# Moving two small statistics operations from VectorE to GpSimd in a graph network kernel

## The chip, the cores and the metric

The kernel runs on one core of one Trainium2 chip. The core has TensorE (matmuls), VectorE and ScalarE (elementwise work, reductions and activations), GpSimd (elementwise work as well, without access to the matmuls' accumulators) and SyncE, which starts the transfers here. Each engine has its own queue of instructions and works through it in order; the engines wait for one another through semaphores. The metric is the time of one execution on the device, in microseconds (us).

## What is computed

128 graphs of 128 nodes with 256 features each go through a first normalisation and three layers of attention over the neighbours, each followed by a feed-forward block; the input is added at the end. Cut to what matters:

```python
def layernorm(x, gamma, beta):
    mu = jnp.mean(x, axis=-1, keepdims=True)
    var = jnp.var(x, axis=-1, keepdims=True)
    return (x - mu) * jax.lax.rsqrt(var + EPS) * gamma + beta
mask = adjacency_matrix.astype(jnp.float32) + jnp.eye(n, dtype=jnp.float32) > 0
x = node_features                      # relu of a plain layernorm of the input
for l in range(attn_w.shape[0]):       # 3 layers
    si = x @ attn_w[l, :d]
    sj = x @ attn_w[l, d:]
    scores = si[:, :, None] + sj[:, None, :] + attn_b[l]
    scores = jnp.where(scores >= 0, scores, 0.2 * scores)
    scores = jnp.where(mask, scores, -jnp.inf)
    attn = jax.nn.softmax(scores, axis=-1)
    agg = jnp.einsum('bij,bjd->bid', attn, x)
    h = layernorm(x + agg, g1[l], beta1[l])
    ff = jax.nn.gelu(h @ W1[l] + b1[l], approximate=False) @ W2[l] + b2[l]
    x = layernorm(h + ff, g2[l], beta2[l])
return x                               # the kernel adds the input to it
```

There are three normalisations: of the input (number 0 in the code), after the attention (1) and after the feed-forward block (2). Each needs, per node, a mean and a variance, then (variance + epsilon) to the power -1/2 and minus the mean times that.

## The kernel before, in words

Four graphs form a group (T = 4), so that a tile is 128 nodes by 4 graphs by 256 features. An item is one group in one layer: 32 groups by 3 layers make 96 items, ordered so that four groups go through the three layers together (12 items to a round of the loop). The program is a software pipeline of slots. In slot s, TensorE runs the feed-forward block of item s in eight pieces (c = 0 to 7), and in between the other stages of its neighbours: the aggregation of item s+1, the transposes of its normalised rows (L435), the attention scores and the transposes of the probabilities of item s+2 (L413). The other engines have a list for each slot, written out by hand in the functions `slot`, with the same eight pieces; nothing reorders it. In four slots out of twelve a new group comes in as item s+4 and its statistics and its mask are made there too.

What the change touches is the way from rows to a normalised tile. VectorE makes statistics of each row (`statistics`, L580, `bn_stats`), and a piece later `aggregates` (L582): four `bn_aggr` (one per graph, L585) that leave mean and variance in `mv`, then one operation that adds epsilon to the variances (`var_eps`, L587) and one that negates the means (`minus_mean`, L588). Both read and write 128x4 numbers in SBUF. Then GpSimd's `inverse_deviation` (L786) raises to the power -1/2 (L789, `rstd`) and multiplies (L791, `shift`). ScalarE (numbers 0 and 1, L491) or GpSimd itself (number 2, `norm_feed`, L815) applies `rstd` and `shift` to the rows.

VectorE calls `aggregates` in three places of a slot: for the attention's norm of item s+1 at c == 0, ahead of the `g_lo` of piece 1 (L573) and the dot products of item s+2 (`dot_products`, L614 and L617); for the feed-forward norm of item s-1 at c == 4, behind the scores (L632), the row maxima (L638) and `minus_max` (L642) of item s+2; and, where a group comes in, for the input's norm at c == 6, ahead of the mask (L601, L604). `feed_residual` at c == 2 makes `res2` (L681).

GpSimd's list in a slot is `inverse_deviation` 1, `h_residual` (L801, L803: two operations on 128x1024 that wait for `norm1`, the dot products and `res2`), `low_X` (L807, `X_lo`), `inverse_deviation` 2, `norm_feed` (four of L815), in some slots the addition of the input to a finished result (`skip_connection`, L836), `inverse_deviation` 0 where a group comes in, and `layer_output` (L827 and L829, two of each).

ScalarE's list has GELU (L481) and the half-precision copy `g_hi` (L486) of each piece, `norm1` (L491) behind piece 2, the copy `X_hi` behind piece 3, the copy of the transposed rows behind piece 4, and behind piece 5 `leaky` (L509) and the exponentials (L514), which wait for `minus_max`.

Of the kernel before, what the change touches and what calls it, by code (L numbers as in the profile page):

```python
# [27 lines left out]
ALU = mybir.AluOpType  # L28
# [101 lines left out]
def gnn_kernel(nc, x, adj, attn_w, attn_b, W1, b1, W2, b2, g1, beta1, g2, beta2, out):  # L130
    with ExitStack() as ctx:
# [335 lines left out]
        def _(act):  # L467
# [26 lines left out]
            def norm_input(r, s):  # L494
                act.wait_ge(rstd_ready[0], group_total(r, s, 2, 2))


                norm_apply(s, 0, x_in[s % 2], X[s % RING], ACT.Relu, x0_ready)

            def norm_attention(r, s):  # L500
                act.wait_ge(rstd_ready[1], total(r, s, 2, 2))
                if later(r, s):
                    act.wait_ge(nT_psum, total(r, s - 1, 1, 1))
                    act.wait_ge(h_res_steps, total(r, s - 1, 2, 2))
                norm_apply(s, 1, res1, norm1, ACT.Identity, norm1_ready)
# [55 lines left out]
        def _(dve):  # L561
# [19 lines left out]

            def aggregates(n, after_8):  # L582

                for t in range(T):
                    dve.bn_aggr(mv[n][:, t, :], bn[n][:, t, :]).then_inc(stat_steps[n], 1)  # L585
                dve.wait_ge(stat_steps[n], after_8)
                dve.tensor_scalar(var_eps[n][:], mv[n][:, :, 1], EPS, None, ALU.add).then_inc(stat_steps[n], 1)  # L587
                dve.tensor_scalar(minus_mean[n][:], mv[n][:, :, 0], -1.0, None, ALU.mult).then_inc(stat_steps[n], 1)  # L588

            def input_statistics(r, s):  # L590
                dve.wait_ge(x_loaded[s % 2], lane_total(r, s))
                if later(r, s):
                    dve.wait_ge(rstd_ready[0], group_total(r, s, 2, 0))
                statistics(0, x_in[s % 2])
# [111 lines left out]
            def slot(r, s):  # L706
# [7 lines left out]
                for c in range(C):  # L714

                    if c == 0 and is_item(r, s + 1):
                        dve.wait_ge(stat_steps[1], total(r, s + 1, 10, 4))
                    if c == 4 and is_item(r, s - 1):
                        dve.wait_ge(stat_steps[2], total(r, s - 1, 10, 4))
                    if c == 6 and starts and not late:  # L720
                        dve.wait_ge(stat_steps[0], group_total(r, s + 4, 10, 4))
                    if isinstance(r, int) and (r, s, c) == (0, -2, 3):
                        dve.wait_ge(stat_steps[0], group_total(0, 1, 10, 4))
                    if is_item(r, s):
                        hidden(r, s, c)
                    if c == 0 and is_item(r, s + 1):
                        aggregates(1, total(r, s + 1, 10, 8))
                    if c == 2 and is_item(r, s - 1):
# [8 lines left out]
                    if isinstance(r, int) and (r, s, c) == (0, -2, 3):  # L737
                        aggregates(0, group_total(0, 1, 10, 8))
                    if c == 3 and is_item(r, s - 1):
# [6 lines left out]
                    if c == 4 and is_item(r, s - 1):  # L746
                        aggregates(2, total(r, s - 1, 10, 8))
                    if c == 5 and is_item(r, s + 1):
# [5 lines left out]
                    if c == 6 and starts and not late:  # L754
                        aggregates(0, group_total(r, s + 4, 10, 8))
                    if c == 6 and is_item(r, s + 2):
# [16 lines left out]
        def _(pool):  # L773
# [12 lines left out]
            def inverse_deviation(s, n, count_stats, count_rstd):  # L786

                pool.wait_ge(stat_steps[n], count_stats)
                pool.tensor_tensor(rstd[n][s % 2][:], var_eps[n][:], minus_half[:], ALU.pow).then_inc(rstd_ready[n], 1)  # L789
                pool.wait_ge(rstd_ready[n], count_rstd)  # L790
                pool.tensor_tensor(shift[n][s % 2][:], minus_mean[n][:], rstd[n][s % 2][:], ALU.mult).then_inc(rstd_ready[n], 1)  # L791
# [17 lines left out]
            def norm_feed(r, s):  # L809

                pool.wait_ge(rstd_ready[2], total(r, s, 2, 2))
                if later(r, s):
                    pool.wait_ge(x_steps, x_total(r, s - 1, 4))
                for t in range(T):
                    pool.tensor_scalar(norm2[:, t, :], res2[:, t, :], rstd[2][s % 2][:, t:t + 1], shift[2][s % 2][:, t:t + 1],  # L815
                                       ALU.mult, ALU.add).then_inc(norm2_ready, 1)
# [21 lines left out]
            def slot(r, s):  # L838
# [3 lines left out]
                if is_item(r, s + 1):  # L842
                    inverse_deviation(s + 1, 1, total(r, s + 1, 10, 10), total(r, s + 1, 2, 1))
                    h_residual(r, s + 1)
                if is_item(r, s + 2):
                    low_X(r, s + 2)
                if is_item(r, s - 1):
                    inverse_deviation(s - 1, 2, total(r, s - 1, 10, 10), total(r, s - 1, 2, 1))
                    norm_feed(r, s - 1)
                if is_item(r, s - 2) and layer_of(s - 2) == L - 1:  # L850
                    skip_connection(r, s - 2)
                if is_item(r, s + 4) and layer_of(s + 4) == 0:
                    inverse_deviation(s + 4, 0, group_total(r, s + 4, 10, 10), group_total(r, s + 4, 2, 1))
                if is_item(r, s - 1) and not (isinstance(r, int) and PER * r + s == ITEMS):
# [24 lines left out]
```

## Time and profile before

| what | value |
|---|---|
| median of three runs | 2462.75 us (2460.89 to 2462.85) |
| the profiled execution's own time | 2464.22 us |
| its span, first to last instruction | 2462.4 us |
| mean granted clock of TensorE | 0.993 of full speed |
| TensorE busy | 2350.7 us, 95% of the span |
| VectorE busy | 2097.8 us, 85% |
| ScalarE busy | 1890.0 us, 77% |
| GpSimd busy | 1701.0 us, 69% |
| transfers, mean rate | 29 GB/s |

The profile is of one execution. Its span leaves out what lies before the first and after the last instruction, 1.8 us here. Busy time is the time in which an instruction of the engine is under way, waiting for a port included; time in which the engine waits for a semaphore is idle time. Engines are named PE (TensorE), DVE (VectorE), ACT (ScalarE), POOL (GpSimd) and SP (SyncE); L12 is line 12 of the program, and an operation is given as output<-inputs by the program's names. Times in the timelines are microseconds from the start of the span.

### The profile page before, as it was taken

To read this page: it belongs to the slowest core of one execution; us is meant where nothing else is said; L and a number is where in the kernel's file an instruction comes from. 1 tells how busy PE (TensorE), PEld (TensorE's weight loads), DVE (VectorE), ACT (ScalarE), POOL (GpSimd) and SP (SyncE) were. 2 spreads that over 40 slices of the span, in tenths; PEclk is the share of its full clock that TensorE was granted. 3 is DMA by queue.
4 is the path that set the end of the run, shared out by engine and by line. 5 is a ranking of instruction groups with operands and counts; after the bars stand their busy time and mean duration, and the time that the engine had idled before them with its cause. 6 is when DMAs were issued, how large, how long until landed. Compare 5 with 4: busy or idle time off the path is not lost.

```text
span 2462.4 us, 47718 instructions
## 1 busy us (share of the span) xinstructions
PE 2350.7 (95%) x16608; PEld 1648.4 (67%) x16608; DVE 2097.8 (85%) x6070; ACT 1890.0 (77%) x3402; POOL 1701.0 (69%) x1540
## 2 busy tenths in 40 slices
PE   3999999999999999999999999999999999999997
PEld 2766666676666666667666666666666666666765
DVE  6778998888988899888988889988898889988884
ACT  4767788877787878787787777877778777878783
POOL 3457677767776767766786667776678676777675
PEclk9999999999999999999999999999999999999998
DMA  5200012000210002100021001200012000110001
GB/s 170 73 1 1 1 44 78 1 1 1 74 48 1 1 14 61 48 1 1 14 78 31 1 1 31 73 18 2 1 44 61 18 2 1 44 52 1 1 1 52
DMA packets 77422, 70.84 MB, mean 29 GB/s; under 512 B 7040, under 2 KB 75648, under 8 KB 77184
## 3 DMA queue, kind: packets, MB, share of 16 engines
q1 hardware_dynamic: 77184, 67.79, 9.1%
q8 instruction: 134, 2.20, 0.4%
q14 instruction: 104, 0.85, 0.1%
HBM read 51.01 MB, written 16.78 MB: 28 GB/s over the span
## 4 chain that ended last, share of the span: by engine, by line
DVE 55%; PE 19%; ACT 13%; issue 10%; POOL 0%; DVEq 0%; POOLq 0%
DVE g_lo L573 11%; DVE bn L580 9%; PE p_pair L383 8%; DVE res L656 6%; DVE dots L614 6%; ACT probs L514 5%; PE p_hid L369 5%; ACT L514 5%; DVE res L681 5%; DVE scores L632 4%; DVE dots L617 4%; PE p_pair L425 3%; DVE row_top L638 3%; DVE minus_max L642 2%; PE p_att L413 2%
## 5 line engine op out<-in xcount | busy, mean ns | idle before, releaser
L383 PE MATMUL p_pair<-w_hi,g_hi 128*128 128x256 f16 x3072 | 839.1, 273 | 0.0
L383 PE MATMUL p_pair<-w_lo,g_hi 128*128 128x256 f16 x3072 | 838.8, 273 | 0.0
L383 PE MATMUL p_pair<-w_hi,g_lo 128*128 128x256 f16 x3072 | 838.8, 273 | 0.0
L481 ACT ACTIVATE p_hid<-p_hid,b_eff 128x512 f32<-128x512 f32 x768 | 504.5, 657 | 328.6 <-PE p_hid L369 327.4
L573 DVE TENSOR_TENSOR g_lo<-p_hid,g_hi 128x512 f16<-128x512 f32 x768 | 527.5, 687 | 239.4 <-ACT g_hi L486 232.9
L801 POOL TENSOR_TENSOR h_res<-norm,g_rows 128x1024 f32<-128x1024 f32 x96 | 227.7, 2372 | 395.8 <-DVE res L681 389.1
L486 ACT ACTIVATE g_hi<-p_hid 128x512 f16<-128x512 f32 x768 | 458.5, 597 | 24.3
L369 PE MATMUL p_hid<-hT_hi,w_hi 128*128 128x512 f16 x1536 | 458.7, 380 | 2.3 <-DVE g_lo L573 2.3
L369 PE MATMUL p_hid<-hT_hi,w_lo 128*128 128x512 f16 x1536 | 458.9, 380 | 0.0
L369 PE MATMUL p_hid<-hT_lo,w_hi 128*128 128x512 f16 x1536 | 458.8, 380 | 0.0
L789 POOL TENSOR_TENSOR rstd<-var_eps,minus_half 128x4 f32<-128x4 f32 x224 | 241.6, 1079 | 307.4 <-DVE minus_mean L588 302.1
L383 PEld LDWEIGHTS p_pair<-w_lo,g_hi 128*128 128x128 f16 x3072 | 301.2, 98 | 107.3 <-issue 0.8
L383 PEld LDWEIGHTS p_pair<-w_hi,g_hi 128*128 128x128 f16 x3072 | 301.2, 98 | 106.2 <-issue 1.0
L383 PEld LDWEIGHTS p_pair<-w_hi,g_lo 128*128 128x128 f16 x3072 | 301.2, 98 | 35.5
L491 ACT ACTIVATE norm<-res,shift,rstd 128x256 f32<-128x256 f32 x384 | 199.3, 589 | 102.0 <-POOL shift L791 102.0
L369 PEld LDWEIGHTS p_hid<-hT_lo,w_hi 128*128 128x128 f16 x1536 | 150.8, 98 | 182.6 <-issue 2.5
L369 PEld LDWEIGHTS p_hid<-hT_hi,w_lo 128*128 128x128 f16 x1536 | 150.7, 98 | 182.5 <-issue 2.2
L580 DVE BATCH_NORM_STATS2 bn<-res 128x6 f32<-128x256 f32 x768 | 268.9, 414 | 3.3
L803 POOL TENSOR_TENSOR h_res<-h_res,res_rows 128x1024 f32<-128x1024 f32 x96 | 226.9, 2363 | 7.5
L587 DVE TENSOR_SCALAR var_eps<-mv 128x4 f32<-128x4 f32 x224 | 213.4, 953 | 7.7
L815 POOL TENSOR_SCALAR norm<-res,rstd,shift 128x256 f32<-128x256 f32 x384 | 209.8, 561 | 10.0
L656 DVE SCALAR_TENSOR_TENSOR res<-p_pair,row_inv,X 128x256 f32<-128x256 f32 x384 | 159.0, 477 | 65.5 <-PE p_pair L425 65.5
(67 smaller groups left out, 3855.2 us busy)
## 6 DMA issues: line engine op xcount, KB each, us to landing
x_in<-in_x SPq DMA_DIRECT2D x32, 512.0 KB, 5.3
x_again<-in_x SPq DMA_DIRECT2D x32, 512.0 KB, 5.1
out<-y_out SPq DMA_DIRECT2D x32, 512.0 KB, 3.3
adj_in<-in_adj SPq DMA_DIRECT2D x32, 256.0 KB, 5.6
w_f<-in_L_gnn_W SPq DMA_DIRECT2D x6, 1024.0 KB, 5.6
attn_rows<-in_L_gnn_attn_w SPq DMA_DIRECT2D x1, 768.0 KB, 5.6
g_rows<-in_L_gnn_g SPq DMA_DIRECT2D x2, 384.0 KB, 8.3
b_rows<-in_L_gnn_b SPq DMA_DIRECT2D x1, 384.0 KB, 7.4
```

The lines of the kernel that those rows point to most:

```text
L369: mm = pe.matmul(p_hid[in_ring(s, c, PF_RING)][:], w[l][:, k, cols], h[i][:, k, :], start=(n == 0), stop=(n == 3 * KD - 1))
L383: mm = pe.matmul(ff_banks(s)[:, t, :], g[i][:, nodes], w[l][:, c, :], start=(c == 0 and t % 2 == 0 and n == 0), stop=(c == C - 1 and n == ...
L481: act.activation(p_hid[k][:], p_hid[k][:], ACT.Gelu, bias=b1_eff[:, l, c:c + 1], scale=1.0 / WSCALE).then_inc(gelu_ready, 1)
L486: act.activation(g_hi[i][:], p_hid[k][:], ACT.Copy).then_inc(g_hi_ready, 1)
L514: act.activation(probs[:, t, :], leaky[:, t, :], ACT.Exp, bias=minus_max[:, t:t + 1], accum_out=row_sum[:, t:t + 1]).then_inc(probs_ready, 1)
L573: dve.tensor_tensor(g_lo[i][:], p_hid[k][:], g_hi[i][:], ALU.subtract).then_inc(g_lo_ready, 1)
L580: dve.bn_stats(bn[n][:, t, :], src[:, t, :]).then_inc(stat_steps[n], 1)
L587: dve.tensor_scalar(var_eps[n][:], mv[n][:, :, 1], EPS, None, ALU.add).then_inc(stat_steps[n], 1)
L656: dve.scalar_tensor_tensor(out=res1[:, t, :], in0=agg_banks(s)[:, t, :], scalar=row_inv[:, t:t + 1], in1=X[s % RING][:, t, :], op0=ALU.mul ...
L789: pool.tensor_tensor(rstd[n][s % 2][:], var_eps[n][:], minus_half[:], ALU.pow).then_inc(rstd_ready[n], 1)
L801: pool.tensor_tensor(h_res[i][:], norm1[:], rows(g1_rows, l, T), ALU.mult).then_inc(h_res_steps, 1)
L803: pool.tensor_tensor(h_res[i][:], h_res[i][:], rows(res_rows, l, T), ALU.add).then_inc(h_res_steps, 1)
```

## The change

The two operations behind the aggregation move from VectorE's `aggregates` to GpSimd's `inverse_deviation`, ahead of the power. VectorE's part ends with `bn_aggr`; its semaphore `stat_steps` counts 8 steps per use instead of 10, and GpSimd's `rstd_ready` counts 4 instead of 2, since GpSimd now waits for its own two operations before it raises to the power. All other waits keep their meaning with the new counts.

```diff
@@ VectorE
-            def aggregates(n, after_8):
+            def aggregates(n):
                 for t in range(T):
                     dve.bn_aggr(mv[n][:, t, :], bn[n][:, t, :]).then_inc(stat_steps[n], 1)
-                dve.wait_ge(stat_steps[n], after_8)
-                dve.tensor_scalar(var_eps[n][:], mv[n][:, :, 1], EPS, None, ALU.add).then_inc(stat_steps[n], 1)
-                dve.tensor_scalar(minus_mean[n][:], mv[n][:, :, 0], -1.0, None, ALU.mult).then_inc(stat_steps[n], 1)
@@ GpSimd
             def inverse_deviation(s, n, count_stats, count_rstd):
                 pool.wait_ge(stat_steps[n], count_stats)
+                pool.tensor_scalar(var_eps[n][:], mv[n][:, :, 1], EPS, None, ALU.add).then_inc(rstd_ready[n], 1)
+                pool.tensor_scalar(minus_mean[n][:], mv[n][:, :, 0], -1.0, None, ALU.mult).then_inc(rstd_ready[n], 1)
+                pool.wait_ge(rstd_ready[n], count_rstd - 1)
                 pool.tensor_tensor(rstd[n][s % 2][:], var_eps[n][:], minus_half[:], ALU.pow).then_inc(rstd_ready[n], 1)
@@ counts, one of each kind
-                act.wait_ge(rstd_ready[1], total(r, s, 2, 2))
+                act.wait_ge(rstd_ready[1], total(r, s, 4, 4))
-                        dve.wait_ge(stat_steps[1], total(r, s + 1, 10, 4))
+                        dve.wait_ge(stat_steps[1], total(r, s + 1, 8, 4))
-                    inverse_deviation(s + 1, 1, total(r, s + 1, 10, 10), total(r, s + 1, 2, 1))
+                    inverse_deviation(s + 1, 1, total(r, s + 1, 8, 8), total(r, s + 1, 4, 3))
```

On VectorE, between the aggregation of the attention's norm (c == 0) and the dot products, this stood before (ISA is the instruction of a dot product and of the read of its sum):

```order
L580 BN_STATS bn<-res 128x6 x3
L573 TENSOR_TENSOR g_lo<-p_hid,g_hi 128x512 [waits g_hi_ready,stat_steps1]
L585 BN_AGGR mv<-bn 128x2 x4
L587 TENSOR_SCALAR var_eps<-mv 128x4 [waits stat_steps1]
L588 TENSOR_SCALAR minus_mean<-mv 128x4
L573 TENSOR_TENSOR g_lo<-p_hid,g_hi 128x512 [waits g_hi_ready]
L614 ISA dots,s_i<-X,attn_rows,attn_b_col 128x256 [waits x_steps]
```

and this stands there now (three lines fewer above it, so that L614 has become L611):

```order
L580 BN_STATS bn<-res 128x6 x3
L573 TENSOR_TENSOR g_lo<-p_hid,g_hi 128x512 [waits g_hi_ready,stat_steps1]
L585 BN_AGGR mv<-bn 128x2 x4
L573 TENSOR_TENSOR g_lo<-p_hid,g_hi 128x512 [waits g_hi_ready]
L611 ISA dots,s_i<-X,attn_rows,attn_b_col 128x256 [waits x0_ready,x_steps]
```

The `g_lo` of piece 1 follows the aggregation directly, and no wait stands between them but the one on ScalarE's `g_hi`.

On GpSimd, from the end of a layer's output to `X_lo` and the feed-forward norm, this stood before:

```order
L829 TENSOR_TENSOR X<-X,beta_rows 128x512 [waits x_steps]
L789 TENSOR_TENSOR rstd_1<-var_eps,minus_half 128x4 [waits stat_steps1]
L791 TENSOR_TENSOR shift_1<-minus_mean,rstd_1 128x4 [waits rstd_ready1]
L801 TENSOR_TENSOR h_res<-norm,g_rows 128x1024 [waits res2_ready,dots_ready,norm1_ready]
L803 TENSOR_TENSOR h_res<-h_res,res_rows 128x1024 [waits h_res_steps]
L807 TENSOR_TENSOR X_lo<-X,X_hi 128x1024 [waits X_hi_ready]
L789 TENSOR_TENSOR rstd_1<-var_eps,minus_half 128x4 [waits stat_steps2]
```

and this stands there now:

```order
L829 TENSOR_TENSOR X<-X,beta_rows 128x512 [waits x_steps]
L786 TENSOR_SCALAR var_eps<-mv 128x4 [waits stat_steps1]
L787 TENSOR_SCALAR minus_mean<-mv 128x4
L789 TENSOR_TENSOR rstd_1<-var_eps,minus_half 128x4 [waits rstd_ready1]
L791 TENSOR_TENSOR shift_1<-minus_mean,rstd_1 128x4 [waits rstd_ready1]
L801 TENSOR_TENSOR h_res<-norm,g_rows 128x1024 [waits res2_ready,dots_ready,norm1_ready]
L803 TENSOR_TENSOR h_res<-h_res,res_rows 128x1024 [waits h_res_steps]
L807 TENSOR_TENSOR X_lo<-X,X_hi 128x1024 [waits X_hi_ready]
L786 TENSOR_SCALAR var_eps<-mv 128x4 [waits stat_steps2]
L787 TENSOR_SCALAR minus_mean<-mv 128x4
L789 TENSOR_TENSOR rstd_1<-var_eps,minus_half 128x4 [waits rstd_ready2]
```

The two operations stand behind the wait for the aggregation (`stat_steps`), and the power waits for them (`rstd_ready`) rather than for VectorE.

## Rows read from the trace of the kernel before

**Rows 1.** The page: TensorE's busy share, and the chain that ended last, by engine.

```profile
PE 2350.7 (95%) x16608; PEld 1648.4 (67%) x16608; DVE 2097.8 (85%) x6070; ACT 1890.0 (77%) x3402; POOL 1701.0 (69%) x1540
...
DVE 55%; PE 19%; ACT 13%; issue 10%; POOL 0%; DVEq 0%; POOLq 0%
```

**Rows 2.** Waits of TensorE: line, whom for, us in total, times, longest us.

```profile
PE p_att L413 <- ACT probs L514: 44.4, 94, 4.5
PE p_pair L435 <- DVE res L681: 20.3, 28, 1.1
```

**Rows 3.** Timeline of TensorE, end of a plain slot: start, duration, operation, [idle before].

```profile
1131.05 0.59 PE L369 MATMUL p_hid<-hT_hi,w_lo 128*128 128x512 f16 x2
1131.49 0.59 PE L369 MATMUL p_hid<-hT_lo,w_hi 128*128 128x512 f16 x2
...
1132.34 0.66 PE L413 MATMUL p_att<-ident,probs 128*128 128x128 f32 x4 [0.25 <-ACT probs L514]
```

**Rows 4.** Timeline of VectorE in the same plain slot.

```profile
1117.63 0.37 DVE L585 BATCH_NORM_AGGREGATE mv<-bn 128x2 f32<-128x6 f32 x4
...
1118.18 0.69 DVE L573 TENSOR_TENSOR g_lo<-p_hid,g_hi 128x512 f16<-128x512 f32 x1
1118.78 0.48 DVE L614 CUSTOM_DVE_ANT_0 dots<-X,attn_rows,attn_b_col 128x256 bf16<-128x256 f32 x1
...
1122.38 1.28 DVE L681 SCALAR_TENSOR_TENSOR res<-p_pair,h_res 128x512 f32<-128x512 f32 x2
...
1125.61 0.69 DVE L573 TENSOR_TENSOR g_lo<-p_hid,g_hi 128x512 f16<-128x512 f32 x1
...
1128.09 0.57 DVE L642 SCALAR_TENSOR_TENSOR minus_max<-row_top 128x4 f32<-128x4 f32 x1
```

**Rows 5.** Timeline of GpSimd in the same plain slot.

```profile
1118.35 1.02 POOL L789 TENSOR_TENSOR rstd<-var_eps,minus_half 128x4 f32<-128x4 f32 x1 [3.11 <-DVE minus_mean L588]
...
1128.60 2.13 POOL L807 TENSOR_TENSOR X_lo<-X,X_hi 128x1024 f16<-128x1024 f32 x1
```

**Rows 6.** Timeline of ScalarE in the same plain slot.

```profile
1119.70 2.08 ACT L491 ACTIVATE norm<-res,shift,rstd 128x256 f32<-128x256 f32 x4 [0.62 <-POOL shift L791]
...
1124.46 0.60 ACT L486 ACTIVATE g_hi<-p_hid 128x512 f16<-128x512 f32 x1
```

**Rows 7.** Timeline of VectorE in an input slot.

```profile
1216.92 1.20 DVE L587 TENSOR_SCALAR var_eps<-mv 128x4 f32<-128x4 f32 x1
...
1218.70 0.47 DVE L614 CUSTOM_DVE_ANT_0 dots<-X,attn_rows,attn_b_col 128x256 bf16<-128x256 f32 x1
...
1222.31 1.27 DVE L681 SCALAR_TENSOR_TENSOR res<-p_pair,h_res 128x512 f32<-128x512 f32 x2
...
1228.01 0.56 DVE L642 SCALAR_TENSOR_TENSOR minus_max<-row_top 128x4 f32<-128x4 f32 x1
```

**Rows 8.** Timeline of GpSimd in the same input slot.

```profile
1211.23 1.43 POOL L789 TENSOR_TENSOR rstd<-var_eps,minus_half 128x4 f32<-128x4 f32 x1 [2.46 <-DVE minus_mean L588]
...
1216.83 1.27 POOL L829 TENSOR_TENSOR y_out<-y_out,beta_rows 128x512 f32<-128x512 f32 x1
...
1228.50 2.13 POOL L807 TENSOR_TENSOR X_lo<-X,X_hi 128x1024 f16<-128x1024 f32 x1
```

**Rows 9.** Timeline, the start-up, the one late `minus_max`.

```profile
159.34 2.12 POOL L807 TENSOR_TENSOR X_lo<-X,X_hi 128x1024 f16<-128x1024 f32 x1
...
159.56 1.92 DVE L642 SCALAR_TENSOR_TENSOR minus_max<-row_top 128x4 f32<-128x4 f32 x1
```

**Rows 10.** Groups by line: operation, count | busy us, mean ns of one | idle before.

```profile
L791 POOL TENSOR_TENSOR shift<-minus_mean,rstd 128x4 f32<-128x4 f32 x224 | 46.8, 209 | 17.6
L815 POOL TENSOR_SCALAR norm<-res,rstd,shift 128x256 f32<-128x256 f32 x384 | 209.8, 561 | 10.0
L587 DVE TENSOR_SCALAR var_eps<-mv 128x4 f32<-128x4 f32 x224 | 213.4, 953 | 7.7
L588 DVE TENSOR_SCALAR minus_mean<-mv 128x4 f32<-128x4 f32 x224 | 35.7, 159 | 0.0
```

More of the change, by code:

```diff
@@ L494, in norm_input @@
             def norm_input(r, s):
-                act.wait_ge(rstd_ready[0], group_total(r, s, 2, 2))
+                act.wait_ge(rstd_ready[0], group_total(r, s, 4, 4))
                 norm_apply(s, 0, x_in[s % 2], X[s % RING], ACT.Relu, x0_ready)
             def norm_attention(r, s):
-                act.wait_ge(rstd_ready[1], total(r, s, 2, 2))
+                act.wait_ge(rstd_ready[1], total(r, s, 4, 4))
                 if later(r, s):
@@ L592, in input_statistics @@
                 if later(r, s):
-                    dve.wait_ge(rstd_ready[0], group_total(r, s, 2, 0))
+                    dve.wait_ge(rstd_ready[0], group_total(r, s, 4, 0))
                 statistics(0, x_in[s % 2])
@@ L716, in slot @@
                     if c == 0 and is_item(r, s + 1):
-                        dve.wait_ge(stat_steps[1], total(r, s + 1, 10, 4))
+                        dve.wait_ge(stat_steps[1], total(r, s + 1, 8, 4))
                     if c == 4 and is_item(r, s - 1):
-                        dve.wait_ge(stat_steps[2], total(r, s - 1, 10, 4))
+                        dve.wait_ge(stat_steps[2], total(r, s - 1, 8, 4))
                     if c == 6 and starts and not late:
-                        dve.wait_ge(stat_steps[0], group_total(r, s + 4, 10, 4))
+                        dve.wait_ge(stat_steps[0], group_total(r, s + 4, 8, 4))
                     if isinstance(r, int) and (r, s, c) == (0, -2, 3):
-                        dve.wait_ge(stat_steps[0], group_total(0, 1, 10, 4))
+                        dve.wait_ge(stat_steps[0], group_total(0, 1, 8, 4))
                     if is_item(r, s):
@@ L726, in slot @@
                     if c == 0 and is_item(r, s + 1):
-                        aggregates(1, total(r, s + 1, 10, 8))
+                        aggregates(1)
                     if c == 2 and is_item(r, s - 1):
@@ L737, in slot @@
                     if isinstance(r, int) and (r, s, c) == (0, -2, 3):
-                        aggregates(0, group_total(0, 1, 10, 8))
+                        aggregates(0)
                     if c == 3 and is_item(r, s - 1):
@@ L746, in slot @@
                     if c == 4 and is_item(r, s - 1):
-                        aggregates(2, total(r, s - 1, 10, 8))
+                        aggregates(2)
                     if c == 5 and is_item(r, s + 1):
@@ L754, in slot @@
                     if c == 6 and starts and not late:
-                        aggregates(0, group_total(r, s + 4, 10, 8))
+                        aggregates(0)
                     if c == 6 and is_item(r, s + 2):
@@ L809, in norm_feed @@
             def norm_feed(r, s):
-                pool.wait_ge(rstd_ready[2], total(r, s, 2, 2))
+                pool.wait_ge(rstd_ready[2], total(r, s, 4, 4))
                 if later(r, s):
@@ L847, in slot @@
                 if is_item(r, s - 1):
-                    inverse_deviation(s - 1, 2, total(r, s - 1, 10, 10), total(r, s - 1, 2, 1))
+                    inverse_deviation(s - 1, 2, total(r, s - 1, 8, 8), total(r, s - 1, 4, 3))
                     norm_feed(r, s - 1)
@@ L852, in slot @@
                 if is_item(r, s + 4) and layer_of(s + 4) == 0:
-                    inverse_deviation(s + 4, 0, group_total(r, s + 4, 10, 10), group_total(r, s + 4, 2, 1))
+                    inverse_deviation(s + 4, 0, group_total(r, s + 4, 8, 8), group_total(r, s + 4, 4, 3))
                 if is_item(r, s - 1) and not (isinstance(r, int) and PER * r + s == ITEMS):
```

## The prediction, made before the changed kernel ran

> **What bounds the kernel now.** I read the page's busy shares and chain first [rows 1]: TensorE is busy 95% of the span, yet the chain of work that ended last lies on VectorE for 55% of it. So TensorE is nearly full, but a loop through the other engines paces it. TensorE's own waits [rows 2] say where: each of the 28 steady slots in which a new graph group comes in (an *input slot*) has a wait on `res2`, and nearly every slot has one on the attention probabilities. The timeline of TensorE [rows 3] gives the room. Pairs of matmuls that follow each other without a gap start 0.44 us apart, so in a slot without input (a *plain slot*) the probabilities' transposes could start at 1131.93; they start at 1132.34. TensorE has 0.41 us to give there.
>
> The loop, in a plain slot [rows 4, 5, 6]: aggregation, the last statistics (L587, L588), `g_lo`, the dot products, `g_lo`, `res2` (ends 1122.38 + 1.28 = 1123.66); then GpSimd does `h_res` (two operations), whose end releases `minus_max`, which releases `leaky` on ScalarE, the exponentials, and TensorE. In an input slot the same chain [rows 7].
>
> One thing decides here. `minus_max` reads SBUF twice and has four columns, but takes 0.57 us [rows 4]: issued at 1128.09, it ends at 1128.66, when GpSimd's second `h_res` operation ends and `X_lo` starts at 1128.60 [rows 5]. It waited for GpSimd, and slipped in between two of its operations. That is a **deadline**: `minus_max` must be issued before `X_lo` starts. It makes it by 1128.60 - 1128.09 = 0.51 us in a plain slot and by 1228.50 - 1228.01 = 0.49 us in an input slot [rows 7, 8]. What happens when it comes late is shown once in the start-up [rows 9]: issued 0.22 us after `X_lo` began, it took 1.92 us and ended with `X_lo`.
>
> **The change, part by part.**
>
> *Off VectorE.* 224 times 0.953 us of `var_eps` and 0.159 us of `minus_mean` go [rows 10], 213.4 + 35.7 = 249 us. Most of it is no work: `var_eps` waits for GpSimd, as in the input slot's 1.20 us up to the end of L829 at 1218.10 [rows 7, 8]. Hardly any of the 249 us shortens the loop. The third of the operations that stands behind `minus_max` (c == 4) lies beside ScalarE's exponentials: worth nothing. In a plain slot the pair between aggregation and `g_lo` costs, from the aggregation's end at 1118.00 to 1118.18, 0.18 us, and 0.09 more because an instruction that waits for nothing starts that much before its neighbour's recorded end, as the dot product does at 1118.78 before `g_lo` ends at 1118.87. I take **0.27 us** for each of the 61 plain slots (96 slots, less 28, less some 7 of the start-up): -16.5 us; the low end is 0.16, -10 us. TensorE's 0.41 us covers it.
>
> *Onto GpSimd.* Each new operation is 128x4. The nearest row is `shift`, the same size on the same engine, 0.209 us [rows 10]; ends are `minus_mean` on VectorE, 0.159, and L815, 0.561, with 64 times the columns. I take 0.20, so a pair and its wait cost 0.36 + 0.08 = 0.44 us. In a plain slot GpSimd may start them at 1118.08, so `pow` starts at 1118.52 (before: 1118.35 [rows 5]). The dot products now start at 1118.51, read two SBUF tensors as `minus_max` does, and I take it that each holds GpSimd's reads off until 0.15 us before its recorded end: the `pow` of the input statistics took 1.43 us [rows 8] instead of 1.02 [rows 5] behind such an operation. So `pow` ends at 1118.51 + 0.48 - 0.15 + 1.02 = 1119.86 and ScalarE's `norm1` starts at 1120.18 instead of 1119.70 [rows 6]. Who waits for that: ScalarE is busy without a gap from `norm1` to the end of `g_hi`, 1125.06 - 1119.70 = 5.36 us; VectorE's `g_lo` follows 0.10 us later and `minus_max` 2.48 us after that (1128.09 - 1125.61 [rows 4]). So `minus_max` is issued no earlier than `norm1` + 7.94 = 1128.12; `X_lo` starts at 1128.60 - 0.27 = 1128.33. The deadline is kept, by 0.21 us, and the plain slot keeps its gain.
>
> *The input slot.* Let T be the end of GpSimd's last layer-output operation (L829, 1218.10 before [rows 8]). Without `var_eps` VectorE reaches the dot products at 1217.4 or sooner (1216.92 less 0.1, and `g_lo`'s 0.6), when GpSimd is still at work, so the wait is not gone: it **moves to the dot products**, which now start at T rather than 1218.70. From dots to the end of `res2` is 1223.58 - 1218.70 = 4.88 us [rows 7], less 0.15 of start that the wait covers: `res2` ends at T + 4.73. `X_lo` follows `res2` by 1228.50 - 1223.58 = 4.92 us, so it starts at **T + 9.65**. On the other side GpSimd adds epsilon and negates after T: 0.40 to `pow`, 1.02, 0.08, 0.20, 0.04 to `norm1` at T + 1.74, and `minus_max` at T + 1.74 + 7.94 = **T + 9.68**, if the dot products never hold GpSimd up. But they run back to back, eight in 3.0 us (1118.78 to 1121.78, where `g_lo`'s 0.6 ahead of `res2` begins [rows 4]), 0.375 us apart; with the additions behind the first, the negation behind the second, `pow` behind the third, `norm1` comes at T + 2.28 and `minus_max` at **T + 10.2**. T drops out: the deadline is missed by 0.03 to 0.57 us whenever the layer's output ends. I take it as missed.
>
> *Its price.* `minus_max` then ends with `X_lo`, 2.13 us long [rows 8]: at T + 11.8 instead of 1228.57. T is 1218.2 if the input statistics' pair costs GpSimd 0.1 us net of its earlier start, 1218.6 if it queues behind both of VectorE's mask operations: 1.4 to 1.8 us per slot; I take 1.5. The 28 slots give **+42 us** (39 to 51). The pair ahead of `norm_feed` delays GpSimd by 0.2 to 0.4 us, which its idle time of 3.11 us [rows 5] and, in input slots, its wait for the input statistics take up; without that cover it would cost as much in each slot.
>
> The sum: -16.5 + 42 = +25.5 us against the profiled 2464.22, so 2489.7. The median of the runs is 1.5 below the profiled time: **2488**. The likeliest case's own range is 2462.75 - 16.5 + 39 = 2485 to 2462.75 - 10 + 51 = 2504.
>
> The Trainium skill, "SBUF — State Buffer", section "Who interferes with whom", agrees that two SBUF inputs contend with GpSimd, but states that whoever issues first holds the pair "for the whole instruction". The trace differs for `pow`: a dot product issued at 1118.78 ran its 0.48 us while `pow` was under way from 1118.35 to 1119.37 [rows 4, 5], where that rule would have held it until 1119.37. By the rule the sum would be the third rival's.
>
> **The rivals.**
>
> 1. *The deadline is kept in the input slots too* (GpSimd's short operations slip between the dot products or hold them up a little). For it: the bare count misses by only 0.03 us. Against: each of three operations would have to pass. Then the input slots gain as well, 0.2 to 0.65 us (T + 4.73 against 1223.58): -6 to -18 us, with -16.5: 2428 to 2440, **2434**. This is the other side: faster. It decides at `minus_max` before T + 9.65. Chance 0.22.
> 2. *The deadline is missed in every slot.* My margin in plain slots is 0.21 us; if the two additions take over 0.3 us each, or `shift` loses one more dot product (0.4 us), it is gone. Then a plain slot's `minus_max` ends at 1128.33 + 2.13 = 1130.46 instead of 1128.66: 61 x 1.8 = +110, with +42: **2615**. Chance 0.10.
> 3. *`pow` holds the dot products for its whole 1.02 us.* Plain slots: dots at 1119.54 instead of 1118.78, 61 x 0.76 = +46; input slots: dots at T + 1.42 = 1219.6 instead of 1218.70, 28 x 0.9 = +25: **2534**. Against it stand rows 4 and 5. Chance 0.03.
> 4. *The input slots split*, half keeping the deadline (two of four also carry GpSimd's skip connection): +21 - 6 - 16.5 = -1.5, **2461**. Chance 0.07.
>
> That the change does nothing is no rival: the order shows the operations gone from VectorE.
>
> **How the numbers follow.** The likeliest case has 0.58. Slower: 0.58 + 0.10 + 0.03 = 0.71; the split gives the same, 0.07; faster 0.22. Faster and slower count from 0.2%, 5 us, about what a measurement of this kernel can tell. The range has to reach rival 1: 2430 to 2510 leaves out rivals 2 and 3 (0.13) and an edge of rival 1.
>
> **What would show it.** Right: in input slots `minus_max` takes some 1.5 to 2.1 us and ends with `X_lo`; the slot is some 1.5 us longer; dots start at the end of L829, the first of them stretched; in plain slots `g_lo` follows the aggregation at once, `minus_max` keeps 0.5 us, the slot is 0.2 to 0.3 us shorter. VectorE's busy time falls, GpSimd's rises by some 90 us (448 x 0.2). Wrong: `minus_max` at 0.5 us in all slots (rival 1) or near 2 us in all (rival 2); GpSimd's additions longer than 0.3 us; dots that do not wait for L829.

## The result and the profile after the change

The changed kernel takes 2529.88 us (median of four runs, 2524.28 to 2531.72) against 2461.82 us (four runs) for the kernel before on the same chip: ratio 1.0273, 95% interval 1.0255 to 1.0291. It is slower by 2.7%. The forecast was 2488 us, with a range up to 2510. The direction was right; the size was not, and the time lies outside the range.

The page of the profiled run (2530.56 us, span 2528.8 us), TensorE's busy share and the chain that ended last:

```profile
PE 2376.6 (94%) x16608; PEld 1665.7 (66%) x16608; DVE 1901.3 (75%) x5622; ACT 1883.4 (74%) x3402; POOL 1834.5 (73%) x1988
...
PE 48%; POOL 17%; ACT 15%; DVE 12%; issue 7%; SPq 0%; DMA 0%; POOLq 0%; DVEq 0%; ACTq 0%
```

VectorE lost 196.5 us of busy time, GpSimd gained 133.5 [rows 1]. Yet the time went up: neither engine's sum was the bound. TensorE's waits (whom for, us in total, times, longest):

```profile
PE p_att L413 <- ACT probs L514: 94.5, 39, 4.5
...
PE p_pair L435 <- DVE res L678: 9.7, 15, 0.7
```

Before, TensorE waited for the probabilities 94 times, 0.47 us on average [rows 2]; now 39 times, 2.4 us on average. Most slots do not wait at all and some wait long. That is the pattern of a deadline that most slots keep and some miss.

**An input slot.** A slot is counted here from the first transpose of the probabilities (L413) to the next slot's first. This one lasts from 1206.72 to 1234.36 us, 27.64 us; before the change the same slot lasted 25.59 us (L413 at 1206.65 and 1232.24). Its end in TensorE's timeline, after the change and then before it:

```profile
1234.36 0.66 PE L413 MATMUL p_att<-ident,probs 128*128 128x128 f32 x4 [2.66 <-ACT probs L514]
```

```profile
1232.24 0.66 PE L413 MATMUL p_att<-ident,probs 128*128 128x128 f32 x4 [0.57 <-ACT probs L514]
```

VectorE in this slot after the change:

```profile
1218.71 0.48 DVE L611 CUSTOM_DVE_ANT_0 dots<-X,attn_rows,attn_b_col 128x256 bf16<-128x256 f32 x1 [1.38 <-POOL X L829]
...
1222.33 1.28 DVE L678 SCALAR_TENSOR_TENSOR res<-p_pair,h_res 128x512 f32<-128x512 f32 x2
...
1229.12 1.56 DVE L639 SCALAR_TENSOR_TENSOR minus_max<-row_top 128x4 f32<-128x4 f32 x1
```

GpSimd in the same slot:

```profile
1211.04 0.64 POOL L786 TENSOR_SCALAR var_eps<-mv 128x4 f32<-128x4 f32 x1 [1.60 <-DVE mv L585]
1211.76 0.37 POOL L787 TENSOR_SCALAR minus_mean<-mv 128x4 f32<-128x4 f32 x1
...
1217.41 1.27 POOL L829 TENSOR_TENSOR X<-X,beta_rows 128x512 f32<-128x512 f32 x1
1218.76 0.53 POOL L786 TENSOR_SCALAR var_eps<-mv 128x4 f32<-128x4 f32 x1
1219.37 0.26 POOL L787 TENSOR_SCALAR minus_mean<-mv 128x4 f32<-128x4 f32 x1
1219.71 1.14 POOL L789 TENSOR_TENSOR rstd<-var_eps,minus_half 128x4 f32<-128x4 f32 x1
...
1228.53 2.13 POOL L807 TENSOR_TENSOR X_lo<-X,X_hi 128x1024 f16<-128x1024 f32 x1
```

ScalarE's `norm1`, which waits for that `rstd` and its `shift`:

```profile
1221.17 2.08 ACT L491 ACTIVATE norm<-res,shift,rstd 128x256 f32<-128x256 f32 x4 [3.34 <-POOL shift L791]
```

Call the end of L829 T again: 1217.41 + 1.27 = 1218.68. The dot products start at T (1218.71), `norm1` starts at T + 2.49, `X_lo` at T + 9.85, `minus_max` is issued at T + 10.44, 0.59 us too late. It ends at 1230.68, with `X_lo` (1230.66), where before it was over 0.07 us after `X_lo` had begun [rows 7, 8].

**A plain slot.** VectorE, then GpSimd:

```profile
1192.61 0.66 DVE L573 TENSOR_TENSOR g_lo<-p_hid,g_hi 128x512 f16<-128x512 f32 x1
...
1193.59 0.42 DVE L614 CUSTOM_DVE_ANT_0 dots<-X,attn_rows 128x256 bf16<-128x256 f32 x1
...
1202.83 0.21 DVE L639 SCALAR_TENSOR_TENSOR minus_max<-row_top 128x4 f32<-128x4 f32 x1
```

```profile
1192.78 0.24 POOL L786 TENSOR_SCALAR var_eps<-mv 128x4 f32<-128x4 f32 x1 [2.26 <-DVE mv L585]
...
1193.42 1.13 POOL L789 TENSOR_TENSOR rstd<-var_eps,minus_half 128x4 f32<-128x4 f32 x1
...
1202.99 2.13 POOL L807 TENSOR_TENSOR X_lo<-X,X_hi 128x1024 f16<-128x1024 f32 x1
```

`minus_max` is issued 0.16 us before `X_lo` (0.51 before the change), still in time, and TensorE's transposes follow without a wait.

**The slot that was not forecast.** Every slot has a layer's output on GpSimd (L827, L829); in two plain slots of twelve the skip connection (L836) comes ahead of it. The first of the two lies right behind a late input slot, has 1.70 us of idle time before its second pair and is on time. The second one is not; it is the slot called "with the skip connection" below. GpSimd there, then VectorE:

```profile
1340.22 0.24 POOL L786 TENSOR_SCALAR var_eps<-mv 128x4 f32<-128x4 f32 x1
...
1344.42 2.35 POOL L836 TENSOR_TENSOR y_out<-y_out,x_again 128x1024 f32<-128x1024 f32 x1
...
1350.66 1.27 POOL L829 TENSOR_TENSOR X<-X,beta_rows 128x512 f32<-128x512 f32 x1
1352.02 0.24 POOL L786 TENSOR_SCALAR var_eps<-mv 128x4 f32<-128x4 f32 x1
1352.35 0.48 POOL L787 TENSOR_SCALAR minus_mean<-mv 128x4 f32<-128x4 f32 x1
...
1362.08 2.13 POOL L807 TENSOR_TENSOR X_lo<-X,X_hi 128x1024 f16<-128x1024 f32 x1
```

```profile
1362.30 1.93 DVE L639 SCALAR_TENSOR_TENSOR minus_max<-row_top 128x4 f32<-128x4 f32 x1
```

None of these rows has idle time before it: from 1340.22 to the end of the second pair GpSimd works without a gap of more than 0.11 us. That pair waits in the queue behind L829 until the dot products run; `minus_mean` starts behind the first of them (1352.35 against 1352.26) and takes 0.48 us, where in the plain slot above it started 0.07 us ahead of it and took 0.23. `minus_max` comes 0.22 us late and takes 1.93.

**The slot behind it.** TensorE waits 2.05 us there, and then its granted clock falls. Slices of 3 us around the wait (after the slice: busy us of TensorE, weight loads, VectorE, ScalarE, GpSimd; granted clock; DMA share; GB/s):

```profile
1362.50:1365.50 3.00, 3.00 (x22) 1.90 (x20) 3.00 (x7) 1.22 (x2) 2.44 (x4) 1.00 0.00 0
1365.50:1368.50 3.00, 0.95 (x6) 0.60 (x4) 0.72 (x1) 2.97 (x10) 2.81 (x6) 0.93 0.00 0
1368.50:1371.50 3.00, 3.00 (x15) 2.13 (x15) 1.01 (x2) 2.96 (x5) 2.92 (x4) 0.51 0.02 5
1371.50:1374.50 3.00, 3.00 (x23) 2.14 (x22) 1.05 (x3) 1.86 (x4) 2.41 (x2) 1.00 0.00 0
```

In the third slice the clock stands at 0.51, its lower level (1.2 GHz), and TensorE does 15 matmuls where the first and the last have 22 and 23. Aggregation starts 6.07 us after the slot's first transpose instead of 4.41, and everything behind it is as late.

The fall does not follow each such wait. In the steady loop 36 slots end with a late `minus_max` and a wait of 2.03 to 2.67 us in TensorE; the clock fell at or within 1.1 us of the end of 20 of these waits, and not behind the other 16. Two input slots in a row, with waits of 2.04 and 2.05 us, in slices of about 3 us behind the wait:

```profile
1262.10:1265.00 2.90, 2.82 (x14) 2.20 (x15) 0.17 (x1) 2.84 (x5) 2.90 (x3) 0.52 0.00 0
...
1290.00:1293.00 3.00, 2.99 (x22) 2.25 (x23) 0.34 (x1) 2.96 (x5) 3.00 (x3) 1.00 0.00 0
```

What decides between the two was not tried.

From the starts of the transposes (L413), slot by slot from the eleventh on, the two profiled runs differ thus:

| slots | before, us each | after, us each | difference in all |
|---|---|---|---|
| 28 input slots | 25.6 | 27.6 to 27.8 | +57.8 |
| 8 plain slots with a late `minus_max` (7 of them with the skip connection) | 24.4 | 26.2 | +14.3 |
| 7 slots at the lower clock behind a late one | 24.4 | 25.7 | +9.4 |
| 42 other slots | 24.4 | 24.1 | -12.3 |
| start-up and end | | | -2.8 |
| sum | | | +66.4 |

The spans differ by 2528.8 - 2462.4 = 66.4 us.

### The profile page after: what moved, and what is told of

Its sections match the earlier page's. It is cut to its first block, busy times and chain, and to the rows that moved or that the text cites. A ratio compares the mean times of both kernels' runs of the same rounds, so it can differ in the third digit from the quotient of the medians.

```text
span 2528.8 us, 47718 instructions
## 1 busy us (share of the span) xinstructions
PE 2376.6 (94%) x16608; PEld 1665.7 (66%) x16608; DVE 1901.3 (75%) x5622; ACT 1883.4 (74%) x3402; POOL 1834.5 (73%) x1988
## 4 chain that ended last, share of the span: by engine, by line
PE 48%; POOL 17%; ACT 15%; DVE 12%; issue 7%; SPq 0%; DMA 0%; POOLq 0%; DVEq 0%; ACTq 0%
PE p_pair L383 21%; PE p_hid L369 19%; POOL rstd L789 3%; PE p_pair L425 3%; ACT norm L491 3%; DVE minus_max L639 3%; ACT p_hid L481 3%; ACT probs L514 2%; ACT L514 2%; POOL y_out L829 2%; POOL y_out L827 2%; DVE scores L629 2%; ACT X_hi L528 2%; ACT g_hi L486 2%; PE p_pair L435 2%
## 5 line engine op out<-in xcount | busy, mean ns | idle before, releaser
L383 PE MATMUL p_pair<-w_hi,g_hi 128*128 128x256 f16 x3072 | 849.5, 277 | 0.0
L383 PE MATMUL p_pair<-w_lo,g_hi 128*128 128x256 f16 x3072 | 849.3, 276 | 0.0
L383 PE MATMUL p_pair<-w_hi,g_lo 128*128 128x256 f16 x3072 | 849.0, 276 | 0.0
L786 POOL TENSOR_SCALAR var_eps<-mv 128x4 f32<-128x4 f32 x224 | 72.4, 323 | 296.1 <-DVE mv L585 283.9
```

The lines of the kernel that those rows point to most:

```text
L383: mm = pe.matmul(ff_banks(s)[:, t, :], g[i][:, nodes], w[l][:, c, :], start=(c == 0 and t % 2 == 0 and n == 0), stop=(c == C - 1 and n == ...
```

## The experiments

Theory A: the time is lost at the deadline, `minus_max` against `X_lo`, and in what TensorE's clock does behind it. Theory B: the moved operations cost their time on GpSimd, spread over all slots; the deadline is a symptom.

Beside these runs the kernel before took 2461.8 to 2463.8 us, so times of different rows can be compared to about 2 us.

| run | kernel | us | ratio to before, 95% |
|---|---|---|---|
| e1 | before, pair of the attention's norm (1) alone moved | 2480.14 | 1.0068 (1.0053 to 1.0083) |
| e2 | before, pairs of the other norms (0, 2) moved | 2470.09 | 1.0029 (1.0018 to 1.0039) |
| e10 | before, pairs of norms 0 and 1 moved | 2503.83 | 1.0167 (1.0152 to 1.0182) |
| e3 | before, one spare reduction ahead of `minus_max` | 2469.87 | 1.0025 (1.0015 to 1.0034) |
| e6 | before, two spare reductions | 2702.95 | 1.0967 (1.0949 to 1.0985) |
| e4 | after, `minus_max` on ScalarE | 2449.93 | 0.9946 (0.9931 to 0.9960) |
| e5 | before, `minus_max` on ScalarE | 2420.91 | 0.9826 (0.9812 to 0.9841) |
| e8 | e1 with `minus_max` on ScalarE | 2427.61 | 0.9855 (0.9840 to 0.9869) |
| e7 | after, filler matmuls one slot too early | 2529.93 | 1.0270 (1.0255 to 1.0286) |
| e9 | after, filler matmuls in the late slots | 2517.03 | 1.0224 (1.0207 to 1.0241) |

**Which pair costs what: e1, e2, e10.** The edit, against the kernel before, lets each norm keep its pair on VectorE or move it; semaphore counts follow.

```diff
+ON_POOL = (1,)
...
-            def aggregates(n, after_8):
+            def aggregates(n, after_8=None):
...
+                if n in ON_POOL:
+                    return
                 dve.wait_ge(stat_steps[n], after_8)
                 dve.tensor_scalar(var_eps[n][:], mv[n][:, :, 1], EPS, None, ALU.add).then_inc(stat_steps[n], 1)
...
+                if n in ON_POOL:
+                    pool.tensor_scalar(var_eps[n][:], mv[n][:, :, 1], EPS, None, ALU.add).then_inc(rstd_ready[n], 1)
+                    pool.tensor_scalar(minus_mean[n][:], mv[n][:, :, 0], -1.0, None, ALU.mult).then_inc(rstd_ready[n], 1)
```

> Only the attention norm's pair (norm 1) goes to GpSimd; norms 0 and 2 stay on VectorE. Theory A (deadline: minus_max must be issued before GpSimd starts X_lo): the layer output still ends at 11.45 us of an input slot, res2 4.93 later at 16.38, X_lo at 21.30, minus_max issued at about 21.9, so all 28 input slots miss and last about 1.5 us longer (+42), the 61 plain slots are 0.28 shorter (-17), the first plain slot behind the skip connection no longer misses: about 2490 us. Theory B (the extra GpSimd time itself is the loss, 133 us of it costing 68): norm 1 has 96 of the 224 pairs, so +29: about 2491 us, but spread evenly, minus_max near 0.25 us everywhere.

> Norms 0 and 2 go to GpSimd, norm 1 stays on VectorE. Theory A: norm1 follows the layer output as before (1.5 us after it), the deadline is kept in every slot, minus_max stays near 0.56 us; input slots only shift with the layer output, 0.5 us later: 28 x 0.5 = +14, plain slots unchanged: about 2476 us. Theory B: 128 of 224 pairs, +39: about 2501 us.

e2 has `ON_POOL = (0, 2)`, e10 `(0, 1)`.

Norm 1's pair makes the input slots late: in e1 `minus_max` is issued 0.59 us after `X_lo` and a late slot takes 27.14 us, 1.54 more than before. VectorE of e1, then GpSimd:

```profile
1209.03 1.56 DVE L647 SCALAR_TENSOR_TENSOR minus_max<-row_top 128x4 f32<-128x4 f32 x1
```

```profile
1208.44 2.13 POOL L816 TENSOR_TENSOR X_lo<-X,X_hi 128x1024 f16<-128x1024 f32 x1
```

Plain slots take 24.08 and the slot with the skip connection is not late. In 8 of the 28 input slots the deadline was kept after all; each of them comes right behind a late one, and TensorE's clock falls at its start or within 1.4 us of it. In five of the eight, `res2` and `X_lo` come 0.7 us later than in the late slots, or more, and `minus_max` no later. So e1 lies 10 us below what was expected; both theories forecast nearly the same total there, and it is the slots that tell them apart. In e2 no slot is late, plain slots stay at 24.37, and two of four input slots take 26.26; it came out below both forecasts, nearer to A.

> The pairs of the input norm and of the norm that every slot waits for on GpSimd, that of the last norm of a layer back on VectorE. If the last norm's pair makes the slot with the skip connection miss the deadline (it pushes GpSimd's whole queue, with y_out and the layer's output in it, 0.56 us back): that slot falls from 26.16 to 24.1 us and the one behind it from 25.74 to 24.1, 8 x 2.1 + 7 x 1.7 = 29 us, so about 2500 us, with the input slots still at 27.6 to 27.8, since the input norm's pair alone puts the end of the layer's output 0.5 us back there. If the miss there comes from the other two: about 2525 to 2530 us, and 26.2 us in that slot.

The slot with the skip connection came down to 24.08 us and the one behind it too; the input slots stayed at 27.6 to 27.8. GpSimd of e10 in that slot, then VectorE:

```profile
1328.89 1.02 POOL L798 TENSOR_TENSOR rstd<-var_eps,minus_half 128x4 f32<-128x4 f32 x1 [0.18 <-DVE minus_mean L593]
...
1338.67 1.27 POOL L838 TENSOR_TENSOR X<-X,beta_rows 128x512 f32<-128x512 f32 x1
1340.45 0.24 POOL L795 TENSOR_SCALAR var_eps<-mv 128x4 f32<-128x4 f32 x1 [0.51 <-DVE mv L588]
...
1350.66 2.13 POOL L816 TENSOR_TENSOR X_lo<-X,X_hi 128x1024 f16<-128x1024 f32 x1
```

```profile
1350.48 0.24 DVE L647 SCALAR_TENSOR_TENSOR minus_max<-row_top 128x4 f32<-128x4 f32 x1
```

The layer's output (L838, L829 in the kernel after) is over 0.51 us before the pair starts, where the kernel after had it over 0.09 us before; `minus_max` is 0.18 us early instead of 0.22 late. So norm 2's pair, far ahead in GpSimd's queue, makes that slot late: 2529.88 - 2503.83 = 26 us. The input norm's pair costs 2503.83 - 2480.14 = 24 us on top of norm 1's: it puts T 0.5 us back in each input slot, and the 8 slots that kept the deadline in e1, worth some 10 us, are late in e10.

**The deadline by itself: e3, e6.** Work is added on VectorE alone, between row maxima and `minus_max`; the results are not used. e6 has both lines, e3 the first alone.

```diff
                 dve.tensor_reduce(row_top[:], scores[:], AX.X, ALU.max, negate=True).then_inc(score_steps, 1)
+                dve.tensor_reduce(row_spare[:], scores[:], AX.X, ALU.max, negate=True)
+                dve.tensor_reduce(row_spare_2[:], scores[:], AX.X, ALU.max, negate=True)
```

> The kernel before, with the row maximum computed a second time into a spare tile ahead of minus_max (about 0.61 us of VectorE; nothing reads it). minus_max has 0.51 us up to X_lo in plain slots and 0.49 in input slots. Theory A: it is now issued about 0.1 us late in every slot and ends with X_lo, 2.1 us later: 90 slots x 2.1 = +190, and more if TensorE's clock falls in the longer stalls: 2640 to 2750 us. Theory B, or no deadline: 0.61 us less the 0.5 that minus_max waited anyway, 90 x 0.1 = +10: about 2472 us.

> The kernel before, with two spare reductions of scores (into tiles that nothing reads) between the row maxima and minus_max. One of them cost 0.07 us in a slot, because minus_max was issued 0.03 us before X_lo began; the second moves it by 0.45 us more. Theory A (a deadline, with GpSimd's operations as in before and nothing moved to GpSimd): minus_max is issued about 0.4 us after X_lo began, lasts 1.7 us and ends with X_lo; every slot is 1.5 to 2.1 us longer, more where TensorE's granted clock falls; 2610 to 2700 us. Rival B (no deadline, each spare reduction costs what it lasts at most): 0.07 to 0.47 us more in each of some 95 slots, 2477 to 2515 us.

In e3 `minus_max` was still issued 0.03 us before `X_lo`, since the reduction moved its issue by 0.47 us in a plain slot, not the 0.61 I had counted on; the run told nothing apart. VectorE of e3:

```profile
1128.52 0.15 DVE L644 SCALAR_TENSOR_TENSOR minus_max<-row_top 128x4 f32<-128x4 f32 x1
```

GpSimd of e3:

```profile
1128.55 2.13 POOL L809 TENSOR_TENSOR X_lo<-X,X_hi 128x1024 f16<-128x1024 f32 x1
```

e6 has the second reduction. VectorE, then GpSimd:

```profile
1230.80 0.68 DVE L642 TENSOR_REDUCE row_spare<-scores 128x4 f32<-128x512 f32 x1
1231.39 1.59 DVE L646 SCALAR_TENSOR_TENSOR minus_max<-row_top 128x4 f32<-128x4 f32 x1
```

```profile
1230.84 2.12 POOL L811 TENSOR_TENSOR X_lo<-X,X_hi 128x1024 f16<-128x1024 f32 x1
```

The first reduction cost 0.07 us in a slot, the second, the same work, 2.0 us and more: plain slots went from 24.43 to 26.45, and to 28.1 where the clock stands at its lower level behind a late one. It is a cliff, with GpSimd's work as before. The run came out 3 us above A's range; by B it would have stayed under 2515 us. So the deadline exists and has this price; how much of the change's loss it explains is for the next runs.

**The deadline taken away: e4, e5, e8.** ScalarE makes `minus_max`.

```diff
-                dve.scalar_tensor_tensor(out=minus_max[:], in0=row_top[:], scalar=SLOPE, in1=row_top[:],
-                                         op0=ALU.mult, op1=ALU.min).then_inc(score_steps, 1)
...
+                act.activation(minus_max[:], row_top[:], ACT.Prelu, scale=SLOPE, alpha=1.0 / SLOPE).then_inc(leaky_ready, 1)
                 act.activation(leaky[:], scores[:], ACT.Prelu, alpha=SLOPE).then_inc(leaky_ready, 1)
```

> The changed kernel with minus_max computed on ScalarE (one Prelu of 128x4 ahead of leaky), so that VectorE has no operation left that GpSimd's X_lo can hold. Theory A: plain slots stay at 24.1; in input slots leaky follows the row maximum at 22.65 instead of 24.0, so a slot lasts about 26.3 instead of 27.65 (28 x 1.4 = -39), the first plain slot behind the skip connection 24.4 instead of 26.2 and the one behind it loses its slow clock (8 x 3.1 = -25): about 2466 us. Theory B: GpSimd's work is unchanged, so the time stays near 2525 us.

> The kernel before, with minus_max alone taken off VectorE: ScalarE forms it from row_top with one small activation ahead of leaky. It is the partner of the kernel after with the same edit (2449.93 us). Theory A (the change lost its time to the deadline of minus_max against X_lo): before keeps that deadline with 0.50 us to spare, so this edit can only take out the 0.35 us that minus_max waits there and give back a ScalarE operation of 0.2 us: plain slots 24.37 to 24.0 to 24.1 us, input slots 25.6 to 25.3; about 2430 to 2440 us. Rival B (the edit is itself worth the 80 us that it took off the kernel after, whatever the deadline): about 2380 us.

> The pair of operations on GpSimd for the second norm of each layer alone (the one that every slot waits for), VectorE keeps the pairs of the other two norms, and minus_max on ScalarE. Theory A: no deadline is left, plain slots as in the kernel after with minus_max on ScalarE, 23.9 us, and the input slots without the 0.6 us that the other norms cost there, 25.5 to 25.7; about 2430 to 2440 us, faster than the kernel before by 1% or so. If the time were GpSimd's busy time, it would stand at 2450 us as that kernel did, or above.

In e4 ScalarE forms `minus_max` in 0.20 us while `X_lo` runs on GpSimd. ScalarE, then GpSimd, in an input slot:

```profile
1192.78 0.20 ACT L509 ACTIVATE minus_max<-row_top 128x4 f32<-128x4 f32 x1 [0.48 <-DVE row_top L636]
```

```profile
1192.19 2.13 POOL L803 TENSOR_TENSOR X_lo<-X,X_hi 128x1024 f16<-128x1024 f32 x1
```

e4 is 80 us faster than the kernel after, and faster than the kernel before, with every moved operation still on GpSimd. It came out 16 us below what A had forecast for it. The same edit on the kernel before gives 43 us: there `minus_max` took 0.56 us in every slot, most of it waiting, and ScalarE needs 0.20. e5 came out 9 us below the forecast, since plain slots went down to 23.90 us and input slots to 25.0 to 25.4. TensorE's waits in e5:

```profile
PE p_pair L435 <- DVE res L677: 24.3, 28, 1.3
...
PE p_att L413 <- ACT probs L515: 9.9, 3, 4.4
```

Only three waits for the probabilities are left. So e5 is the fastest, faster than both kernels; and e4 against e5 says what the move costs without any deadline: 29 us, nearly all of it 0.9 us in each input slot. e8, with norm 1's pair alone, lies between, 7 us above e5 and 2 below its forecast: 0.34 us in each input slot is the price of `norm1` waiting for GpSimd's pair behind T, and the other 0.58 goes with T, which lies 0.5 to 0.6 us further back in e4 than in e8. So of the 68 us that the change cost, about 29 do not need the deadline, and about 39 come with it and with the clock behind it. Theory B is right to that extent, though its cost lies in the input slots and not in all.

**TensorE's clock: e7, e9.** Nine matmuls on operands at hand; the transposes overwrite their result. This is e9; e7 had `LATE_SLOTS = (8, 9, 10, 11, 1)`.

```diff
+LATE_SLOTS, FILL = (9, 10, 11, 0, 2), 9
...
             def transpose_probs(r, s):
+                if s - 2 >= 5 and (s - 2) % PER in LATE_SLOTS:
+                    pe.wait_ge(score_steps, total(r, s, 6, 4))
+                    for _ in range(FILL):
+                        pe.matmul(p_att[:].rearrange("p t n -> p (t n)"), w1_hi[0][:, 0, :P], w1_hi[0][:, 0, :TN], start=True, stop=True)
```

> The kernel after, with nine matmuls of 512 columns added on TensorE in five slots of twelve (the four input slots and the one with the skip connection behind them), issued once the scores are there and before the transposes of the probabilities; their result is overwritten. They fill most of the 2.2 to 2.8 us in which TensorE waits for a late minus_max. If the fall of the granted clock comes from that wait: the granted clock stays at its upper level behind these slots, the slot behind the skip connection falls from 25.74 to about 24.1 us in seven or eight places, the input slots by 0 to 0.2 us, and the run takes about 2512 to 2520 us. If the clock falls for another reason: slots as in the kernel after, 2528 to 2535 us. minus_max stays late (1.5 to 1.9 us) by both.

The slots were off by one: two punctual slots in twelve got fillers, each longer by 1.8 us for it, and the last late input slot of each group got none. Gains and losses cancelled, but the profile had its use: the lower clock came behind 7 of the 8 late slots without fillers, and behind none of the 21 with them. The slot with the skip connection was on time here, since the slot before it had become longer.

> The kernel after with the same nine matmuls, but now in front of the transposes that end the slots with a late minus_max; the run before had them one slot too early (a filled slot on time became 1.8 us longer, and no slot that was late and filled was followed by the lower granted clock). If the fall of the clock comes from the wait in TensorE: no half-clock episodes in the steady loop, the slot behind the skip connection 25.74 to about 24.1 us, seven or eight times, -12 us, input slots shorter by 0 to 0.2 us, -3 us: 2510 to 2520 us. If the clock falls for another reason: 2528 to 2535 us, with the 25.74 us slots still there. By both, minus_max stays late and the input slots stay at 27.6 us.

In the steady loop of e9 the clock stays at its upper level, and the slot behind the skip connection takes 24.08 us. The same place as in the slices above, in e9:

```profile
1358.10:1361.10 3.00, 2.90 (x16) 1.43 (x15) 0.75 (x1) 2.97 (x10) 2.81 (x6) 1.00 0.00 0
1361.10:1364.10 3.00, 3.00 (x24) 2.11 (x23) 0.98 (x2) 2.96 (x5) 2.92 (x4) 1.00 0.00 0
```

13 us came back although TensorE did more work and `minus_max` was as late as ever. So the fall of the clock comes from the wait, where it comes at all, and costs about 13 us of the 68 (a little more, since one punctual slot at the end got fillers too and became 1.8 us longer).

## Why the prediction was wrong

**Right:** the deadline, the place where it is missed, and that plain slots without GpSimd's extra work keep it (0.16 to 0.19 us to spare, forecast 0.21) and gain (0.29 us, forecast 0.27). The dot products start at T, and `minus_max` ends with `X_lo`. The first rival, deadline kept in input slots, did not happen in the kernel after; in e1 it did, in 8 of 28, by that side effect. `pow` did not hold the dot products: in the plain slot above, one of 0.42 us ran at 1193.59, while `pow` was under way from 1193.42 to 1194.55. That the measured 2529.88 lies near the third rival's 2534 is therefore chance.

The Trainium skill, "SBUF — State Buffer", section "Who interferes with whom", says that a VectorE instruction with two SBUF inputs contends with a GpSimd instruction that reads SBUF, and, in its item on VectorE's 2-port modes, that whoever issues first has the shared ports "for the whole instruction". Taken for two inputs as well, this fits `X_lo`, which held a late `minus_max` off to its end each time (1.56 of its 2.13 us in the input slot); it does not fit `pow`.

Two of the signs were wrong on their own account. "`minus_max` keeps 0.5 us" in plain slots did not go with a margin of 0.21: it took 0.21 to 0.25 us there. And the first dot product behind T was not stretched (0.48 us).

**Wrong, in three steps:**

1. *"I take 1.5" us for the price of an input slot.* It is 57.8 / 28 = 2.06. The step that put T at 1218.2 to 1218.6 and `minus_max`'s end at T + 11.8 is the mis-sized one, and even its upper bound, 51 us, was too low: the input norm's pair queued behind both of VectorE's mask operations (0.64 and 0.37 us for what takes 0.24 and 0.23 elsewhere), so T moved by 0.51 us within the slot, the top of my bound. From T on the price was 1.53 us more than before, against 11.8 - 10.47 = 1.33 in my working; part of that is that the dot products no longer wait for the port but for a semaphore, so that the 0.15 us which I let the wait cover was not covered (`res2` ends at T + 4.93, not T + 4.73). e1, where T has not moved, shows 1.54.
2. *"The pair ahead of `norm_feed` delays GpSimd by 0.2 to 0.4 us, which its idle time of 3.11 us ... take up."* True of a plain slot like the one read. I had taken 61 plain slots as alike; two in twelve have the skip connection ahead of the layer's output in GpSimd's queue. Before the change GpSimd was idle there for 0.80 us, not 3.11, and the trace showed it:

```profile
1318.27 1.02 POOL L789 TENSOR_TENSOR rstd<-var_eps,minus_half 128x4 f32<-128x4 f32 x1 [0.80 <-DVE minus_mean L588]
```

In the slot with the skip connection the pair ahead of `norm_feed` put the end of L829 from 9.61 (e10) to 10.19 us behind the slot's first transpose, 0.58 us, more than the 0.51 us of idle time that e10 has there. The slot missed by 0.22 us, +1.8 us each. e10 shows that this one pair, with what follows from it, costs 26 us.
3. *No term for TensorE's clock.* I took each slot's loss as its own. Behind 20 of the 36 waits of 2 us or more the clock came down, and the next slot paid. In input slots that costs 0.2 us at most; in a plain slot 1.7 us (25.74 against 24.08). e9 puts it at 13 us.

Set against my sum of +25.5, the profiled runs' +66.4 has 16 us more in the input slots, 14 in late plain slots, 9 in slots at the lower clock, and 4 less gain in plain slots, of which fewer were left; 3 us came back at the two ends. The additions on GpSimd were taken at 0.20 us; undisturbed they are 0.24 and 0.23, with 0.08 between them, and with their waits for a port:

```profile
L786 POOL TENSOR_SCALAR var_eps<-mv 128x4 f32<-128x4 f32 x224 | 72.4, 323 | 296.1 <-DVE mv L585 283.9 <-DVE res_rows L764 4.5
L787 POOL TENSOR_SCALAR minus_mean<-mv 128x4 f32<-128x4 f32 x224 | 59.2, 265 | 18.2
```

That explains GpSimd's 133.5 us more of busy time against 90 forecast. "GpSimd's additions longer than 0.3 us" stood among the signs of being wrong, and on average `var_eps` was; in plain slots it was not, and the longer ones in input slots are step 1.

One late plain slot of the eight, at 2056 us, has no skip connection; one `g_lo` of VectorE came 0.35 us later there than in the slot before. The same slot is late in e7 and e9. What held it up was not tried and stays open; it shows how thin a margin of 0.18 us is.

## What to carry to other kernels

When a small VectorE operation with two SBUF inputs slips in just ahead of a long GpSimd operation, its margin is a number to be tracked like a buffer: half a microsecond of GpSimd work upstream can cost 2 us, and a busy-time balance won't show it. Count the slots by what the queue holds in each, not by the one that was read, and price a new wait of TensorE with what its clock does in the next slot. The better edit was to take the small operation away from the contended engine: `minus_max` on ScalarE made the kernel before 1.7% faster, and showed that the moved pair has no benefit of its own.

## What the runs showed of the hardware

- A two-input VectorE operation issued 0.03 us before a GpSimd operation of 2.13 us takes 0.15 us (e3); issued 0.55 us after its start, it takes 1.59 (e6). The one reduction of 128x512 that lies between the two runs is worth 2702.95 - 2469.87 = 233 us.
- `pow` of 128x4 on GpSimd, 1.13 us long, did not hold off a VectorE operation with two SBUF inputs, which ran its 0.42 us within it (after, 1193.42 to 1194.55).
- A wait of 2.05 us in an otherwise full TensorE was followed by a granted clock of 0.51 in the slice of 3 us behind it (so it went behind 20 of 36 such waits); where 0.95 us of matmuls in the slice of the wait became 2.90 by fillers, it stayed at 1.00. Doing useless work there shortened the run by 13 us.
